# Token mixing on quarters of the TensorE array: four 64x64 matmuls in the place of one 128x128

## The reference, cut to what matters

```python
# layer 0: GCN, two products and two batch norms over all 8192 tokens
agg = jnp.einsum('nm,bmd->bnd', A_hat, features)            # mixes the 64 nodes of a batch
h = relu(batchnorm(agg.reshape(-1, d) @ W1.T + b1, g1, be1))
out = batchnorm(h @ W2.T + b2, g2, be2)
# layer 1: Chebyshev term, attention over the 64 nodes, MLP
xp = jnp.einsum('mn,bnf->bmf', L_norm, x)                   # mixes the nodes
# layer 2: two graph products, then LSTM cells over windows of nodes
h = relu(jnp.einsum('ts,bsh->bth', adj, x @ Wg0 + bg0))     # mixes the nodes
h = relu(jnp.einsum('ts,bsh->bth', adj, h @ Wg1 + bg1))     # mixes the nodes
# layer 3: graph attention (softmax over the nodes, then attention @ Wh)
```

## Time and profile before

| | us |
|---|---|
| median of 3 runs | 2279.95 |
| lowest and highest run | 2275.58, 2283.84 |
| the profiled execution | 2281.25 |
| span of its core, first to last instruction | 2279.1 |
| mean granted TensorE clock, share of full speed | 0.969 |

### The profile page before, as it was taken

One profiled execution on the slowest core, in us unless ns is written; L12 is line 12 of the kernel. 1 busy time (PEld: TensorE's weight loads), 2 busy tenths in 40 slices (PEclk: granted clock), 3 DMA queues, 4 the chain that ended last, 5 costly groups with the idle time before them and its releaser, 6 DMA issues.

```text
span 2279.1 us, 56488 instructions
## 1 busy us (share of the span) xinstructions
PE 2075.3 (91%) x21573; PEld 1789.4 (79%) x21573; DVE 1661.8 (73%) x4873; ACT 1363.2 (60%) x3387; POOL 189.2 (8%) x242
## 2 busy tenths in 40 slices
PE   7979669999999998999999989999899999999985
PEld 5544358889788987888888978898888888888875
DVE  6879566777777776777777777777777777777744
ACT  4647345656565756666566656575656556666654
POOL 0000000010101010101010110101010101010100
PEclk9989789999999999999999999999999999999998
DMA  7767200000100001000100010000000010000000
GB/s 263 272 244 287 99 2 19 11 11 2 39 3 11 11 2 40 11 11 2 40 11 11 2 39 3 19 2 10 32 11 11 1 40 11 11 2 11 2 10 10
DMA packets 37904, 92.68 MB, mean 41 GB/s; under 512 B 2545, under 2 KB 27121, under 8 KB 33393
## 3 DMA queue, kind: packets, MB, share of 16 engines
q1 hardware_dynamic: 37616, 88.86, 11.1%
HBM read 55.29 MB, written 33.55 MB: 39 GB/s over the span
## 4 chain that ended last, share of the span: by engine, by line
PE 34%; DVE 22%; issue 19%; ACT 10%; POOL 4%; DVEq 0%; DMA 0%; ACTq 0%; POOLq 0%
PE ps L257 10%; PE ps L259 9%; PE ps L258 9%; POOL rstd L1494 4%; DVE stats L1534 3%; ACT pool_mem L1368 2%; DVE pool_mem L1680 2%; ACT pool_mem L1402 2%; PE ps L1081 1%; DVE pool_mem L1664 1%; ACT pool_mem L1410 1%; DVE pool_mem L1666 1%; DVE hl_a L1586 1%; DVE mv L1538 1%; PE ps L1072 1%
## 5 line engine op out<-in xcount | busy, mean ns | idle before, releaser
L1402 ACT ACTIVATE pool_mem<-ps,lstm_b 128x128 f32<-128x128 f32 (+2 forms) x1248 | 438.4, 415 | 289.6 <-PE ps L259 272.9
L257 PE MATMUL ps<-hl_a,w_hi 128*128 128x256 f16 (+2 forms) x1984 | 466.4, 258 | 19.9 <-DVE hl_a L791 12.9
L258 PE MATMUL ps<-hl_a,w_hi 128*128 128x256 f16 (+2 forms) x1984 | 465.9, 258 | 0.0
L259 PE MATMUL ps<-hl_a,w_lo 128*128 128x256 f16 (+2 forms) x1984 | 465.7, 258 | 0.0
L257 PE MATMUL ps<-hl_b,w_hi 128*128 128x168 f16 (+2 forms) x1408 | 361.5, 265 | 22.8 <-issue 18.5
L258 PE MATMUL ps<-hl_b,w_hi 128*128 128x168 f16 (+2 forms) x1408 | 361.1, 265 | 0.0
L259 PE MATMUL ps<-hl_b,w_lo 128*128 128x168 f16 (+2 forms) x1408 | 360.3, 264 | 0.5 <-issue 0.5
L1494 POOL TENSOR_TENSOR rstd<-ve,nhalf 128x2 f32<-128x2 f32 x224 | 184.4, 826 | 1836.8 <-DVE ve L1541 1836.8
L257 PE MATMUL ps<-pool_mem,w_hi 128*128 128x128 f16 (+2 forms) x1536 | 313.0, 234 | 0.8
L258 PE MATMUL ps<-pool_mem,w_hi 128*128 128x128 f16 (+2 forms) x1536 | 312.8, 234 | 0.0
L259 PE MATMUL ps<-pool_mem,w_lo 128*128 128x128 f16 (+2 forms) x1536 | 312.8, 234 | 0.0
(11 more groups left out here) (240 smaller groups left out, 4598.2 us busy)
## 6 DMA issues: line engine op xcount, KB each, us to landing
xa<-in_x SPq DMA_DIRECT2D x32, 512.0 KB, 5.2
h_scratch<-pool_mem SPq DMA_DIRECT2D x16, 1024.0 KB, 4.3
pool_mem<-h_scratch SPq DMA_DIRECT2D x16, 1024.0 KB, 7.4
pool_mem<-in_wpack SPq DMA_DIRECT2D x16, 704.0 KB, 4.1
o_scratch<-act_in SPq DMA_DIRECT2D x16, 512.0 KB, 3.0
act_in<-o_scratch SPq DMA_DIRECT2D x16, 512.0 KB, 6.1
out<-xb SPq DMA_DIRECT2D x16, 512.0 KB, 3.0
row<-in_rows SPq DMA_DIRECT2D x1, 1408.0 KB, 11.0
```

What stands on the lines that cost most here:

```text
L257: nc.tensor.matmul(o, l[0], r[0], start=first, stop=False, skip_group_check=True)
L258: nc.tensor.matmul(o, l[0], r[1], start=False, stop=False, skip_group_check=True)
L259: return nc.tensor.matmul(o, l[1], r[0], start=False, stop=last, skip_group_check=True)
L1402: op = nc.scalar.activation(gates[s][:, g, m * w:(m + 1) * w], ps[s][:, g, m * w:(m + 1) * w], ACT.Tanh, bias=lstm_b[:, bias:bias + 1], sc ...
```

## The change

A helper `quarters` replaces each 128x128 mixing matmul by four of 64x64. The stationary operand is a batch's 64 tokens (rows `n`) by 64 features (columns `c`), the moving one the 64x64 matrix alone (`matrix[n, n]`). The zero quarters of the block diagonal matrix are no longer streamed. Each of the four stands on its own quarter of the array: the batch picks the half of the rows, `c` the half of the columns.

The two batches of a block go to two different PSUM banks, since both halves of the rows would else write the same bank. So `xp`, `m0` and `m1` of half 0 take banks 0 and 1 and those of half 1 banks 2 and 3 (`MIX_BANK`), and the aggregate has batch 0 in bank 0 and batch 1 in bank 1. ACT and DVE read both banks through a view whose runs are 64 elements long, and write such runs. `gcn_first` writes `BANK_B` (0, 2) rather than `BANK_LATE` (0, 1), and `gcn_relu` reads that. `gcn_second` waits for the low part of half 0 of `m1` as well as of its own half. Ahead of each mix and aggregate PE increments a semaphore (`begun`) that nobody waits for; the waits for the operands now stand on that instruction, in PE's instruction stream ahead of the matmuls.

```diff
+        def quarters(to, of, matrix):
+            for f in range(KT):
+                for c in (slice(0, P // 2), slice(P // 2, P)):
+                    for batch in range(P // NODES):
+                        n = slice(batch * NODES, (batch + 1) * NODES)
+                        mm = nc.tensor.matmul(to(f, batch)[c, :], of(f)[n, c], matrix[n, n], start=True, stop=True)
+            return mm
...
                 def agg_high(s, n):
                     act.wait_ge(agg_ps[s], n)
-                    nc.scalar.copy(hl_a[s][:, 0, :, :], by_feature(s, 0)).then_inc(agg_hi[s], 1)
+                    nc.scalar.copy(by_batch(hl_a[s][:, 0, :, :]), aggregated(s)).then_inc(agg_hi[s], 1)
...
-                    for f in range(KT):
-                        for b in range(BLK):
-                            mm = nc.tensor.matmul(ps[s][:, f, b * P:(b + 1) * P], xa[s][:, b, f * P:(f + 1) * P],
-                                                  gcn_t[:, :], start=True, stop=True)
+
+                    pe.sem_inc(begun, 1)
+                    for b in range(BLK):
+                        mm = quarters(lambda f, batch: ps[s][:, batch, (f * BLK + b) * NODES:(f * BLK + b + 1) * NODES],
+                                      lambda f: xa[s][:, b, f * P:(f + 1) * P], gcn_t)
                     mm.then_inc(agg_ps[s], 1)
...
+            MIX_BANK = {"xp": [(0, 1), (2, 3)], "m0": [(0, 1), (2, 3)], "m1": [(0, 1), (2, 3)]}
...
                 def mix(s, n, h, src, matrix, which):
...
+                    banks = MIX_BANK[which][h]
+
+                    pe.sem_inc(begun, 1)
+                    for b in range(HALF):
+                        mm = quarters(lambda f, batch: ps[s][:, banks[batch], (f * HALF + b) * NODES:(f * HALF + b + 1) * NODES],
+                                      lambda f: src[s][:, h * HALF + b, f * P:(f + 1) * P], matrix)
                     mm.then_inc(feat_ps.of(s, h), 1)
...
-                    dense(s, h, hl_a[s], h * HTOK, "wg0", BANK_LATE[h], (sums[:, 0:P], gbias[:, 0, :])).then_inc(tok_ps.of(s, h), 1)
+                    dense(s, h, hl_a[s], h * HTOK, "wg0", BANK_B[h], (sums[:, 0:P], gbias[:, 0, :])).then_inc(tok_ps.of(s, h), 1)
...
                 def gcn_second(s, n, h):
+                    pe.wait_ge(*feat_lo.at(s, n, 0, "m1"))
                     pe.wait_ge(*feat_lo.at(s, n, h, "m1"))
```

More of the change, by code:

```diff
@@ L293, in build @@
             adj_in = psem("adj_in")
+            begun = psem("agg_begun")
             vec_in = psem("vec_in")
@@ L334, in build, with aggregated, by_batch @@
                                     spare[:, P:2 * P])
+            def aggregated(s):
+                return ps[s][:, 0:2, :].rearrange('p c (j n) -> p j c n', n=NODES)
+            def by_batch(buf):
+                return buf.rearrange('p k (b c n) -> p (k b) c n', c=P // NODES, n=NODES)
             hid_bank = [[2, 3, 0, 1], [2, 0, 1, 2]]
@@ L887, in build @@
             x_in = x3_in
+            begun = pctx.enter_context(nc.semaphore("mix_begun"))
             o_in, out_stored, y_ok = psems("o_in"), psems("out_stored"), psems("y_ok")
@@ L971, in fea, with feat, like_feat @@
                 return ps[s][:, bank, :].rearrange("p (k n) -> p k n", k=KT)
+            def feat(s, h, which):
+                if which in MIX_BANK:
+                    first, second = MIX_BANK[which][h]
+                    return ps[s][:, first:second + 1:second - first, 0:HTOK].rearrange("p c (k b n) -> p k b c n", k=KT, b=HALF)
+                return fea(s, FEAT_BANK[which][h])
+            def like_feat(buf, which):
+                return buf.rearrange("p k (b c n) -> p k b c n", b=HALF, n=NODES) if which in MIX_BANK else buf
             def half_row(name):
@@ L1076, in mix @@
                 def mix(s, n, h, src, matrix, which):
-                    bank = FEAT_BANK[which][h]
-                    for f in range(KT):
-                        for b in range(HALF):
-                            mm = nc.tensor.matmul(fea(s, bank)[:, f, b * P:(b + 1) * P],
-                                                  src[s][:, h * HALF + b, f * P:(f + 1) * P], matrix[:, :],
-                                                  start=True, stop=True)
+                    banks = MIX_BANK[which][h]
[3 more added lines that the diff above has]
+                                      lambda f: src[s][:, h * HALF + b, f * P:(f + 1) * P], matrix)
                     mm.then_inc(feat_ps.of(s, h), 1)
@@ L1337, in high @@
                 def high(s, n, h, which):
-                    src = fea(s, FEAT_BANK[which][h])
+                    src = feat(s, h, which)
                     act.wait_ge(*feat_ps.at(s, n, h, which))
@@ L1345, in high @@
                         func, scale = ACT.Copy, 1.0
-                    nc.scalar.activation(FEAT_DST[which][s][:, 0, :, tokens(h)], src, func, scale=scale)\
+                    nc.scalar.activation(like_feat(FEAT_DST[which][s][:, 0, :, tokens(h)], which), src, func, scale=scale)\
                         .then_inc(feat_hi.of(s, h), 1)
@@ L1388, in gcn_relu @@
                     act.wait_ge(*tok_ps.at(s, n, h, "gcn"))
-                    nc.scalar.activation(t[s][:, blocks(h), :], tok(s, BANK_LATE[h]), ACT.Relu, scale=UNSCALE)\
+                    nc.scalar.activation(t[s][:, blocks(h), :], tok(s, BANK_B[h]), ACT.Relu, scale=UNSCALE)\
                         .then_inc(taken.of(s, h), 1)
@@ L1583, in low @@
                     dve.wait_ge(*feat_hi.at(s, n, h, which))
-                    hi, lo = (FEAT_DST[which][s][:, c, :, tokens(h)] for c in range(2))
-                    src = h1_full(s, h) if which == "h1" else fea(s, FEAT_BANK[which][h])
+                    hi, lo = (like_feat(FEAT_DST[which][s][:, c, :, tokens(h)], which) for c in range(2))
+                    src = h1_full(s, h) if which == "h1" else feat(s, h, which)
                     nc.vector.tensor_tensor(lo, src, hi, ALU.subtract).then_inc(feat_lo.of(s, h), 1)
```

5 lines of the change are left out of this document (2 added, 3 removed).

## The result

| | us |
|---|---|
| median before, 15 runs | 2276.90 |
| median after, 15 runs | 2290.84 (2283.25 to 2297.09) |
| ratio after to before, 95% interval (the ratio of the two medians is 1.0061) | 1.0049 (1.0038 to 1.0060) |
| the profiled execution after | 2290.84, span 2288.7 |
| mean granted clock, before and after | 0.969, 0.961 |

The account below looks back on a forecast made before the run. It took PE to bound passes one and three. Terms of 5.3 (pass one) and 7.4 (pass three) make 12.7 us, taking the profiled 2281.25 to 2268.5; less 1.3 for the median, 2267 us, range 2250 to 2298.

Parts of the forecast that it names:

- What bounds the kernel: Passes one and three: PE is busy 132.57 of 134 and 229.37 of 244 us, so less PE work saves time.
- The group time of 0.056: Mixes and aggregates: four quarter matmuls run at once, 0.056 us a group, against 0.112 for a full record.
- rival B: Mixes and aggregates: quarters don't run four at a time, a group takes 0.112 us plus switches; 2291 us, chance 0.13.
- its extreme: Mixes and aggregates: quarter matmuls run one at a time, a half-mix takes 1.8 us instead of 0.9; 2378 us, chance 0.04.
- Rival D: Passes one and three: mixes occupy PE's array less, so the clock falls once more each round; 2290 us, chance 0.06.
- Entering and leaving: Around a row of quarters: switching tiling costs about 0.10 + 0.05 us in, 0.10 out; a half-mix takes 0.84, not 1.00.
- What reaches the end, pass one: Pass one: only aggregate 0 counts, 0.66 us a round, 5.3 us in 8 rounds.
- What reaches the end, pass three: Pass three: Chebyshev halves 0.63, stream 0's `mix0` 0.25 and `mix1` 0.35 a round; three quarters of 9.8 arrive, 7.4 us.
- ACT and DVE at nothing: ACT and DVE reads of two banks in runs of 64 elements: no added cost, 0 us.
- the term for everything outside the mixes: Rest of a pass three round: later waits, some 14 us of 244, were taken not to move with PE.
- C: Passes one and three: other waits absorb the savings and one of two terms stays; 2275 to 2277 us, chance 0.21.
- E: Savings counted as absorbed come back, as waits at L1548 and L1680 move too; twice the terms, 2252 us, chance 0.14.

Follow-up runs that it names:

- e9: Changed kernel, half 0 of the very first Chebyshev mix computed twice, putting 64 instructions ahead of the loop (242 left): 2273.15 us, ratio 0.9976.
- e2: Pass three alone changed to quarters, pass one as in the kernel before: 2278.22 us, ratio 0.9993.
- e1: Pass one alone changed (aggregates on quarters), pass three as in the kernel before: 2272.32 us, ratio 0.9969.
- e11: Kernel before, half 0 of the very first Chebyshev mix computed five times (253 instructions left): 2282.99 us, ratio 1.0022.
- e12: Changed kernel, pause partly filled by three repeated matmuls twice a round, plus 64 instructions ahead of the loop (236 left): 2263.32 us, ratio 0.9939.
- e7: Changed kernel, three matmuls repeated twice a round ahead of the 1.35 us wait for ScalarE (44 left): 2289.36 us, ratio 1.0044.
- e8: Kernel before, three matmuls repeated twice a round ahead of the 1.35 us wait for ScalarE (55 left): 2280.47 us, ratio 1.0006.
- e5: Changed kernel, half 0 of the very first Chebyshev mix computed five times, loop untouched (50 left): 2294.18 us, ratio 1.0057.
- e10: Kernel before, three matmuls of the very first Chebyshev mix issued once more, so 49 instructions are left: 2298.93 us, ratio 1.0082.

## Why the prediction was wrong, point by point

- *What bounds the kernel*: right for pass one, where less work of PE's came out as time. In pass three it hardly did.
- *The group time of 0.056*: right. Two aggregates, 32 groups, last 2.10 us, (2.10 - 0.22)/32 = 0.059. All four quarters work at once, so rival B and its extreme did not come true. The rule of "TensorE: Matmul & The Clock Gate" of the Trainium skill, Part 3, that spoke against the change doesn't hold here: two of the quarters share their rows, and yet a group takes 0.059. That the median after, 2290.84, is B's 2291 and D's 2290 is chance.
- *Entering and leaving*: right, 0.83 for 0.84 in all.
- *What reaches the end, pass one*: right, 5.3 forecast. The profiled execution after is 6.65 us ahead by then, of which 2 are from the first round, with nothing beside it; other executions with the same pass one are 4.7 to 6.8 ahead. In the medians 5.5 arrive: e9 is 5.1 under e2, with 0.45 of added work.
- *What reaches the end, pass three*: wrong. The 7.4 us, or 0.92 a round, are mis-sized. At the mixes themselves some 0.7 us a round is won: the stretch at `mix0` and `mix1` of stream 0 gave 0.6, as reckoned, but the Chebyshev mixes, for which I had 0.63, only 0.1. They were thought to be free of waits, since no wait stood on either side; the time was lost at later ones. And where the jump back is equally cheap in both, even of the 0.7 at most 0.15 a round is left (0.7 us in five rounds, e9 against e1 and e11). Some of it is seen to be given back right at the jump, where e9 and e2 wait 14.7 us in five and e1 13.2; why they wait longer is open.
- *ACT and DVE at nothing*: right. In pass three ACT's copy has a median of 588 to 597 ns after and 589 to 597 before, DVE's subtraction 684 to 685 and 685; in pass one they have 1012 and 1219 after, 1012 and 1225 before.
- *The step that failed* is the term for everything outside the mixes, put at nothing without a reason. First the jump back. The prediction calls 3.1 us each PE's "two largest groups" of waits in a round. The answer behind the earlier trace rows has a larger one at its head, and a small one at its foot, which neither the rows nor the sum took up:

```profile
PE ps L257 <- issue: 3.3, 1, 3.3
...
PE ps L259 <- issue: 0.2, 1, 0.2
```

  These are the two waits for instructions at the jump. The change moved the loop in the program, from 61 to 50 instructions left, and the second wait went from 0.09 to 0.94 us a jump. With it came the clock, the other cost: 68.3 us at the lower level in five rounds instead of 41.0. Placement alone, with the loop untouched, makes 17.8 us in five rounds (e9 and after) and 17.7 in the medians, and 2267 + 17.7, with the 7.4 of pass three that didn't arrive, is 2292; 2290.84 was measured.
- *Rival D*, to which I gave 0.06, has the right kind of cost and the wrong reason. I priced a fall of the clock well (1.6, measured 1.67), but put the reason into the mixes, which would keep the array less occupied. None of the low stretches shown above holds a mix, and e2 and e9 with quarters have the same 34.1 us at the lower clock as e1 without. The falls come at pauses that were there before. D's own sign, a mean clock under 0.96, didn't show either: it is 0.961.
- *Sums of the rivals*: C says that one of the two terms stays and takes off 5 or 3, but the terms are 5.3 and 7.4, so it should read 2273 to 2275. E says twice the terms, which is 25.4, and takes off 28. D's sixteen stretches of 1.6 are 26 and give 2293, not 2290. None of them changes the forecast.
- *The range* ended at 2298 and so held the time, but by the spread of B and D, not by the mechanism. That was luck.

The nearest thing to the forecast is e9: the same loop with its place put right runs 0.24% (5.0 us) under the kernel before. That is pass one's term and no more; the 7.4 of pass three aren't in it. Its profiled execution, span 2267.1, is 12.0 under the span of before, but it is the fastest of its eleven and before's is slower than its median.

The Trainium skill, "Runtime: NRT & Kernel Launch", section Instruction fetch mechanics, says that instructions are refilled in blocks of 256 and that a taken branch to a target outside what is held forces a fetch. The rows agree, with 16.4 KB a packet and 2.5 to 3.3 us a jump. "TensorE: Matmul & The Clock Gate" of the Trainium skill, section HAM oscillation, tells of a loop that pays a fall of the clock in every turn because of a pause that each turn has. That is what after's rounds do, at three places, though the page's example waits longer than the 1.35 us seen here.

## What to carry to other kernels

A change to a loop's code, or to the code ahead of it, also moves the loop in the program, and where the jump back has to fetch the loop's instructions, it can cost more or less for that reason alone: here 17 to 18 us (0.7%) in five rounds between the best and the worst place of the same loop. So read the engine's waits for its own instructions at the loop's end in both profiles before judging a change of a few tenths of a per cent, and try the same code shifted. When PE waits in every round for the same thing, a few repeated matmuls ahead of the wait can keep the clock up: worth 9.8 us here with the loop well placed (e12 against e9), and nothing while they moved it to a bad place (e7, e8). And a saving of half a microsecond in a long round needn't show at all: compare kernels whose jump back costs the same before calling it a gain.

## What the runs showed of the hardware

- Four 64x64 fp32 matmuls, on the four quarters of the array, run at the same time: 0.059 us for a group of four records, against 0.112 for the one record of 128x128 that it replaces.
- There is a second wait for instructions after the jump back, on average none with 69 or more instructions left in the piece, 0.09 us at 61, 0.93 at 55, 0.94 to 1.05 at 49 and 50, 1.97 at 45 and 2.12 at 44. The packet of the next piece started 0.2 to 0.9 us after the first matmul behind the jump, and 2.2 to 3.0 us later its instructions ran.
- The clock did not fall on one pause and fell on the same pause, with the same records, in the other kernel. Rounds settled at nearly equal lengths, 245.3 to 246.0 us in after, e5 and e10 and 242.1 to 242.7 in e1 and e11.
- The spread of after's 15 runs goes with the granted clock: the three lowest times (2283.25 to 2286.11) have 0.961 to 0.963, the three highest (2293.22 to 2297.09) 0.958 to 0.960.
